# A fused Mamba and local-attention kernel: the time step by one Softplus activation

## The chip, the cores and the metric

The kernel runs on one core of one Trainium2 chip. The metric is the device time of one execution in microseconds, from launch to end; the profile's span is the stretch from the first to the last instruction inside it.

## The reference

Two branches read the same 4096 x 256 input and their results are added. The first is a Mamba block (inner width 512, 16 states, rank 16):

```
x_conv = silu(conv4(x @ in_proj_x) + conv_b);  z = x @ in_proj_z
dt_lr, B, C = split(x_conv @ x_proj.T)
dt  = softplus(dt_lr @ dt_proj_w.T + dt_proj_b)         # 4096 x 512
dA  = exp(dt * A);  dBx = (dt * x_conv) * B             # 4096 x 512 x 16
h_t = dA_t * h_(t-1) + dBx_t;  y_t = sum_n h_t * C_t
out = ((y + x_conv * D) * silu(z)) @ out_proj.T
```

The second is two layers of local attention (8 heads of 64, windows of 128 tokens, l2-normalised and rotated q and k, softmax) with a gated feed-forward of width 682 (gelu). Only the line that makes `dt` is computed in another way by the change.

## The kernel before

Everything is fp32. The 4096 tokens are worked in 8 chunks of 512. A chunk's Mamba state work is 64 units, one for each of 16 states and 4 tiles `j` of 128 channels (`NJ = 4`). A unit is a 128 x 512 tile: ScalarE makes `dA` = Exp(dt * A) (L963), VectorE makes dBx for two units at once (L749), runs the recurrence as one scan (L756) and multiplies two units by C (L763); GpSimd saves the last state (L1177) and issues a DMA that accumulates the product into `ysum` in HBM (L1193). `dA` is a ring of 8 tiles. Its tile is free for ScalarE's next Exp only when the accumulating DMA that reads it has landed (`act.wait_ge(*added[jb]...)`). `hb` is a ring of 4. The attention and feed-forward of the same chunk run between the units: 8 attention blocks `a` (2 layers x 4 windows) and 4 feed-forward halves `f`.

Each engine executes one fixed list in order. The lists are written out as strings: a FIRST list (chunk 0 and the start of chunk 1), an ORDER list that is run six times, and a LAST list; a word names a stage and its arguments, and each `+` says that it belongs to a later chunk. `heads(7)` is the transposition of q and k of attention block 7, `s` the scores (L1390 mask, L1396 product), `m` their row maximum on VectorE (L847), `e` the softmax exponentials on ScalarE (L1098), `turn` the rotation and norm (VectorE L824 to L842, ScalarE L1073), `h` the feed-forward's hidden tile (gelu L1130 on ScalarE, L899 on VectorE), `z` the Silu gate (L1144), `silu` the convolution's (L1019). TensorE writes into 7 PSUM banks taken in turn (`ring`); a bank is free when a named reader has read it.

The time step of a chunk passes through these stages:

- TensorE `xdbl` (L1351), ScalarE copy (L1033), TensorE `dt(j)` (L1358) into a PSUM bank.
- ScalarE `dt(j)` (L1038): dt_sb = Identity(PSUM + bias), which also frees the bank.
- VectorE `dt(half)` = `clip` (L805): u_sb = min(dt_sb, 40), for two tiles.
- ScalarE `softplus(half)`: an explicit load of a table that serves Exp and Ln (L1042), Exp in place on two tiles (L1045), Ln(x + 1) in place on two tiles (L1048).
- VectorE `u(half)`: dt_sb = max(dt_sb, u_sb) on two tiles (L811), then u_sb = dt_sb * x_conv (L816).
- The units of a half wait for `dt_ready` (ScalarE's Exp) and `u_ready` (VectorE's dBx).

Of the kernel before, what the change touches and what calls it, by code (L numbers as in the profile page):

```python
# [76 lines left out]
+k(3) +pT(2,0) +pT(2,1) +pT(2,2) +pT(2,3) +o(2,0) +o(2,1) +v(3) +hT(0) +o(2,2) +o(2,3) +h(0,0) +h(0,1)
+h(0,2) +h(0,3) +heads(3) +h(0,4) +h(0,5) +s(3,0) +s(3,1) +rb(2) ++xnT(0) +w2(0) ++xnT(1) +wo(2) +pT(3,0)
+pT(3,1) +pT(3,2) +x2T(0) +rb(3) +pT(3,3) +o(3,0) ++in(0) +o(3,1) ++in(1) ++in(2) +o(3,2) +o(3,3) ++in(3)
+q(4) +wo(3) +k(4) +sh(1) ++conv(0) ++conv(1) ++conv(2) ++conv(3) +heads(4) +hT(1) +q(5) +h(1,0) +h(1,1)  # L80
+h(1,2) +h(1,3) +h(1,4) +h(1,5) +s(4,0) +s(4,1) +k(5) +v(4) ++xdbl +w2(1) +pT(4,0) +rb(4) +pT(4,1) +pT(4,2)
# [9 lines left out]
+scan w2(3) ++norm(0) branch(1) +scan +scan +scan +scan +m(1,0) +m(1,1) +o(0) +m(1,2) +m(1,3) +scan +rinv(1)
+turn(q,2) +turn(k,2) +scan +scan +o(1) +wo(0) +u(1) +turn(q,3) +m(2,0) +wo(1) +m(2,1) +m(2,2) +m(2,3)
+stats(0) +scan ++norm(1) +turn(k,3) +scan +scan +scan +h(0,0) +h(0,1) +h(0,2) +h(0,3) +scan +scan +rinv(2)
+h(0,4) +h(0,5) +m(3,0) +m(3,1) +scan +o(2) +m(3,2) +m(3,3) +scan +scan +rinv(3) +w2(0) +scan +wo(2) +scan
+scan +scan +o(3) +scan +scan +wo(3) +turn(q,4) +turn(k,4) +stats(1) +scan +scan +scan +scan +scan +scan
+turn(q,5) +scan +scan +h(1,0) +h(1,1) +h(1,2) +h(1,3) +scan +h(1,4) +h(1,5) +m(4,0) +m(4,1) +scan +m(4,2)
+m(4,3) +turn(k,5) +rinv(4) +scan +scan +gate(0) +w2(1) +scan +scan +scan +scan ++dt(0) +m(5,0) +o(4)
+m(5,1) +m(5,2) +m(5,3) +scan +rinv(5) +turn(q,6) +turn(k,6) +scan +o(5) +scan +wo(4) +wo(5) +stats(2) +scan
+m(6,0) +m(6,1) +m(6,2) +m(6,3) +scan +scan +turn(q,7) +turn(k,7) +h(2,0) +h(2,1) +scan +rinv(6) +h(2,2)
+h(2,3) +scan +h(2,4) +scan +h(2,5) ++u(0) +scan  # L100
# [2 lines left out]
+dA heads(7) +dA v(7) e(7,0) e(7,1) e(7,2) e(7,3) +q(0) pT(7,0) pT(7,1) pT(7,2) pT(7,3) +k(0) +dA rb(7)
+turn(q,0) +turn(k,0) +v(0) +heads(0) +dA +dA +q(1) hn(3) +e(0,0) +e(0,1) +pT(0,0) +k(1) +e(0,2) +e(0,3)
last(3) hT(3) +dt(2) +dA +dA +dt(3) +dA +dA +dA h(3,0) h(3,1) h(3,2) +turn(q,1) h(3,3) h(3,4) h(3,5) +rb(0)
+start(0) +dA +dA +turn(k,1) +dA +dA +pT(0,1) +pT(0,2) +softplus(1) +dA +pT(0,3) +heads(1) +dA +dA +z(0)
# [1493 lines left out]
```

## Time and profile before

| | |
|---|---|
| median of 3 runs | 2244.7 us (2244.4 to 2245.45) |
| profiled execution, whole | 2240.71 us |
| its span | 2238.9 us |
| TensorE matmul busy | 2058.0 us (92%) |
| VectorE busy | 2016.8 us (90%) |
| ScalarE busy | 1680.9 us (75%) |
| GpSimd busy | 928.2 us (41%) |
| mean granted TensorE clock | 0.976 of full |

Busy time counts the union of an engine's instructions; waits are idle time. The matmul engine's ends are modelled, so its busy share is an upper view of its load. A row of a group of instructions gives the line, engine, operation, tiles and count, then busy us and mean ns of one, then the idle time just ahead of them and what ended it.

### The profile page before, as it was taken

How to read it: one execution, taken by the hardware profiler on the slowest of the kernel's cores; microseconds unless marked ns; L12 is line 12 of the kernel's file. 1: busy time of each engine (PE TensorE's matmuls, PEld its weight loads, DVE VectorE, ACT ScalarE, POOL GpSimd, SP SyncE). 2: the span in 40 equal slices, each digit the busy share in tenths (PEclk: the TensorE clock that was granted, in tenths of full speed). 3: DMA queues.
4: the chain of work that ended last, by engine and by line, in shares of the span. 5: the costliest groups of instructions: out<-in, count | busy, mean ns of one | idle time of the engine just before them, and what ended most of it. 6: DMA issues, size and time to landing. Idle time of an engine off the chain costs nothing. (4 is left out here: it accounts for less than half of the span.)

```text
span 2238.9 us, 37820 instructions
## 1 busy us (share of the span) xinstructions
PE 2058.0 (92%) x10944; PEld 1318.1 (59%) x10944; DVE 2016.8 (90%) x2804; ACT 1680.9 (75%) x4087; POOL 928.2 (41%) x1086
## 2 busy tenths in 40 slices
PE   6789989999899999999899998999989999898897
...
GB/s 142 145 152 194 188 155 183 180 205 175 161 196 178 188 161 157 220 187 169 193 136 189 208 187 165 157 179 200 181 166 196 173 197 167 163 162 217 115 200 54
DMA packets 113131, 388.52 MB, mean 174 GB/s; under 512 B 11408, under 2 KB 32272, under 8 KB 94368
## 3 DMA queue, kind: packets, MB, share of 16 engines
...
## 5 line engine op out<-in xcount | busy, mean ns | idle before, releaser
L756 DVE TENSOR_TENSOR_SCAN hb<-dA,state,hb 128x512 f32<-128x512 f32 x512 | 668.3, 1305 | 34.7 <-ACT dA L963 20.5
L1177 POOL COPY state<-hb 128x2 f32<-128x2 f32 x256 | 223.5, 873 | 638.5 <-DVE hb L756 638.2
L963 ACT ACTIVATE dA<-dt_sb,amat 128x512 f32<-128x512 f32 x512 | 344.3, 720 | 81.8 <-DMA ysum<-dA 80.8
L1193 POOL DMA_DIRECT2D ysum<-dA x256 | 220.2, 883 | 382.6 <-DVE dA L763 272.6
L1465 PE MATMUL ring<-hT,w 128*128 128x256 f32 (+1 forms) x1536 | 354.5, 388 | 17.4 <-ACT hT L1119 16.9
L1465 PEld LDWEIGHTS ring<-hT,w 128*128 128x128 f32 (+1 forms) x1536 | 272.6, 182 | 94.5 <-ACT hT L1119 26.0
L749 DVE TENSOR_TENSOR hb<-u_sb,bc 128x1024 f32<-128x1024 f32 x256 | 311.3, 1216 | 2.0 <-DMA bc<-bc_rows 1.9
L763 DVE TENSOR_TENSOR dA<-hb,bc 128x1024 f32<-128x1024 f32 x256 | 307.2, 1200 | 0.0
L1073 ACT ACTIVATE rot<-rot,rnorm 128x64 f32<-128x64 f32 x1024 | 257.2, 339 | 50.8 <-POOL rnorm L1262 50.7
L1098 ACT ACTIVATE probs<-ring,nmax 128x256 f32<-128x256 f32 x512 | 235.6, 483 | 55.5 <-DVE nmax L847 55.1
L1262 POOL TENSOR_TENSOR rnorm<-rnorm,powers 128x8 f32<-128x8 f32 x128 | 230.2, 1799 | 23.5 <-POOL rnorm L1259 23.5
L847 DVE TENSOR_REDUCE nmax<-ring 128x2 f32<-128x512 f32 x256 | 163.3, 681 | 41.9 <-PE ring L1396 41.6
L1477 PE MATMUL ring<-w,hid 128*128 128x256 f32 (+1 forms) x768 | 192.2, 395 | 0.3 <-issue 0.3
L1373 PE MATMUL ring<-wqkv,x2T 128*128 128x512 f32 x384 | 183.0, 606 | 9.6 <-ACT xconv L1019 9.0
L1106 ACT ACTIVATE pT<-ring 128x512 f32<-128x512 f32 x256 | 146.2, 598 | 53.6 <-PE heads_out L1417 28.1
L1373 PE MATMUL ring<-wqkv,xnT 128*128 128x512 f32 x384 | 181.6, 603 | 0.1
L1477 PEld LDWEIGHTS ring<-w,hid 128*128 128x128 f32 (+1 forms) x768 | 135.3, 189 | 55.4 <-issue 42.2
L1417 PE MATMUL heads_out<-pT,V 128*64 128x128 f32 x2048 | 152.7, 282 | 10.7 <-ACT pT L1106 5.6
L1316 PE MATMUL ring<-ident,probs 128*128 128x128 f32 x1024 | 142.1, 279 | 16.6 <-ACT probs L1098 6.9
L1396 PE MATMUL ring<-kT,qT 64*128 64x256 f32 x1024 | 156.0, 426 | 0.0
L1316 PEld LDWEIGHTS ring<-ident,probs 128*128 128x128 f32 x1024 | 115.2, 142 | 63.3 <-issue 41.5
L1417 PEld LDWEIGHTS heads_out<-pT,V 128*64 128x64 f32 x2048 | 110.9, 137 | 65.3 <-issue 64.6
...
## 6 DMA issues: line engine op xcount, KB each, us to landing
bc<-bc_rows SPq DMA_DIRECT2D x128, 1024.0 KB, 5.8
ysum<-dA POOLq DMA_DIRECT2D x256, 512.0 KB, 7.2
...
```

Of the source, the lines that this page charges most:

```text
L749: dve.tensor_tensor(hb[:, slot:slot + 2, :], u_pair, bc[:, g % 2, :, 0, :], ALU.mult)\
L756: dve.tensor_tensor_scan(hb[:, k % H_RING, :], dA[:, k % DA_RING, :], hb[:, k % H_RING, :], state[:, k:k + 1], ALU.mult, ALU.add).then_inc ...
L763: dve.tensor_tensor(dA[:, out:out + 2, :], hb[:, slot:slot + 2, :], bc[:, g % 2, :, 1, :], ALU.mult).then_inc(hC_ready.sem, 1)
L963: act.activation(dA[:, k % DA_RING, :], dt_sb[:, j, :], ACT.Exp, scale=amat[:, n:n + 1]).then_inc(dA_ready.sem, 1)
L1073: act.activation(rot[:, i, h * DH:(h + 1) * DH], rot[:, i, h * DH:(h + 1) * DH], ACT.Copy, scale=rnorm[:, i * HEADS + h:i * HEADS + h + 1] ...
L1098: act.activation(probs[:, g, odd, :], bank(it, ("s", a, p))[:, hh * 256:(hh + 1) * 256], ACT.Exp, bias=nmax[:, 2 * p + hh:2 * p + hh + 1], ...
L1262: pool.tensor_tensor(rnorm[:, part], rnorm[:, part], powers[:, part], ALU.pow).then_inc(rnorm_ready.sem, 1)
L1316: m = pe.transpose(bank(it, name)[:, b * P:(b + 1) * P], block_, ident[:, :])
L1373: m = pe.matmul(bank(it, name)[:, :], (x2T if l else xnT)[:, ft, off:off + WIN], wqkv[:, ft, i * 512:(i + 1) * 512], start=(ft == 0), stop ...
L1417: m = pe.matmul(obank[odd * DH:(odd + 1) * DH, g * WIN:(g + 1) * WIN], V[:, a // NW, s, h * DH:(h + 1) * DH], pT[:, g % 2, 2 * odd + s, :] ...
L1465: m = pe.matmul(bank(it, ("h", f, i))[0:rows, part * 256:(part + 1) * 256], w1[:, ft, col:col + rows], hT[:, ft, :], start=(ft == 0), stop ...
L1477: m = pe.matmul(bank(it, ("w2", f))[:, v * D:(v + 1) * D], hid[0:rows, i, v * WIN:(v + 1) * WIN], w2[0:rows, i, :], start=(i == 0), stop=( ...
```

## The change

`clip`, the Exp, the Ln, the maximum, the table load by hand and four of the five semaphores of the chain go. ScalarE's stage `dt(j)` now writes dt_sb = Softplus(PSUM + bias) and signals `dt_ready`; TensorE's bank is freed by that. VectorE's `u(half)` keeps only the product, and takes over the wait for the old chunk's last reader of `u_sb` that `clip` had. The function text no longer names a table; the build puts a table load in front of an activation whose function is not in the loaded table, as it does for the other activations before.

```diff
-            def clip(half):
-                for j in range(half * JH, half * JH + JH):
-                    dve.wait_ge(*dtv_ready.at(it, j + 1))
-                    dve.wait_ge(*dBx_ready.at(it - 1, (half + 1) * SUMS // HALVES))
-                    dve.tensor_scalar(u_sb[:, j, :], dt_sb[:, j, :], 40.0, None, ALU.min).then_inc(dtmin_ready.sem, 1)
-
             def u(half):
 
-                for j in range(half * JH, half * JH + JH):
-                    dve.wait_ge(*dtlog_ready.at(it, j + 1))
-                    dve.tensor_tensor(dt_sb[:, j, :], dt_sb[:, j, :], u_sb[:, j, :], ALU.max)\
-                       .then_inc(dt_ready.sem, 1)
                 for j in range(half * JH, half * JH + JH):
                     dve.wait_ge(*dt_ready.at(it, j + 1))
                     dve.wait_ge(*xconv_ready.at(it, j + 1))
+                    dve.wait_ge(*dBx_ready.at(it - 1, (half + 1) * SUMS // HALVES))
                     dve.tensor_tensor(u_sb[:, j, :], dt_sb[:, j, :], xconv[:, j, :], ALU.mult).then_inc(u_ready.sem, 1)
...
-            def dt_out(j):
+            def softplus(j):
                 act.wait_ge(*filled(it, ("dt", j)))
                 act.wait_ge(*dA_ready.at(it - 1, (j // JH + 1) * UNITS // HALVES))
-                act.activation(dt_sb[:, j, :], bank(it, ("dt", j))[:, :], ACT.Identity,
-                               bias=par[:, C_DTB + j:C_DTB + j + 1]).then_inc(dtv_ready.sem, 1)
-
-            def softplus(half):
-                act.preload_act_table_set("natural_log_exp_and_others")
-                for j in range(half * JH, half * JH + JH):
-                    act.wait_ge(*dtmin_ready.at(it, j + 1))
-                    act.activation(u_sb[:, j, :], u_sb[:, j, :], ACT.Exp).then_inc(dtexp_ready.sem, 1)
-                for j in range(half * JH, half * JH + JH):
-                    act.wait_ge(*dtexp_ready.at(it, j + 1))
-                    act.activation(u_sb[:, j, :], u_sb[:, j, :], ACT.Ln, bias=1.0).then_inc(dtlog_ready.sem, 1)
+                act.activation(dt_sb[:, j, :], bank(it, ("dt", j))[:, :], ACT.Softplus,
+                               bias=par[:, C_DTB + j:C_DTB + j + 1]).then_inc(dt_ready.sem, 1)
```

All fifteen order lists are written anew in the same diff: the same stages without the removed ones, in another order. The places that matter below, cut from them:

```diff
 ACT_ORDER (head)
-+dA heads(7) +dA v(7) e(7,0) e(7,1) e(7,2) e(7,3) +q(0) pT(7,0) pT(7,1) pT(7,2) pT(7,3) +k(0) +dA rb(7)
+heads(7) v(7) +dA +dA e(7,0) e(7,1) +q(0) e(7,2) e(7,3) +k(0) pT(7,0) pT(7,1) pT(7,2) pT(7,3) +dA rb(7)
...
 ACT_ORDER (the z gates)
-+start(0) +dA +dA +turn(k,1) +dA +dA +pT(0,1) +pT(0,2) +softplus(1) +dA +pT(0,3) +heads(1) +dA +dA +z(0)
-+z(1) +z(2) +z(3) +dA +dA +dA +e(1,0) +e(1,1) +e(1,2) +e(1,3) +q(2) +k(2) +v(1) +pT(1,0) +pT(1,1) +turn(q,2)
++pT(0,0) +dA +dA +dA +turn(q,1) +turn(k,1) +pT(0,1) +heads(1) +dA +dA +z(0) +pT(0,2) +dA +pT(0,3) +z(1)
++z(2) +z(3) +start(1) +dA +dA +dA +e(1,0) +e(1,1) +e(1,2) +e(1,3) +q(2) +pT(1,0) +k(2) +v(1) +pT(1,1)
...
 ACT_ORDER (tail)
-+h(2,0) +h(2,1) ++softplus(0) +h(2,2) +h(2,3) +h(2,4) +h(2,5) +pT(6,0) +pT(6,1) +dA +dA +pT(6,2) +turn(q,7)
-+rb(6) +turn(k,7) ++skip(0) +pT(6,3) ++dA ++dA
++e(6,3) +k(7) +pT(6,0) +turn(q,7) +turn(k,7) +h(2,0) +h(2,1) +h(2,2) +h(2,3) +rb(6) +h(2,4) +h(2,5) +dA +dA
+++dA ++skip(0) +pT(6,1) ++dA +pT(6,2) +last(2) +pT(6,3)
...
 PE_FIRST (head)
-xnT(0) xnT(1) in(0) in(1) in(2) in(3) conv(0) conv(1) conv(2) conv(3) q(0) xdbl dt(0) dt(1) k(0) heads(0)
+xnT(0) xnT(1) k(0) q(0) in(0) in(1) conv(0) conv(1) in(2) in(3) conv(2) conv(3) heads(0) xdbl q(1) dt(0)
...
 DVE_FIRST (head)
-norm(0) norm(1) +norm(0) turn(q,0) dt(0) +norm(1) turn(k,0) u(0) scan scan m(0,0) m(0,1) m(0,2) m(0,3) scan
+norm(0) norm(1) turn(q,0) turn(k,0) +norm(0) m(0,0) m(0,1) u(0) m(0,2) m(0,3) turn(q,1) scan scan rinv(0)
...
 ACT_FIRST (where dt is made)
-dt(0) dt(1) k(0) softplus(0) turn(k,0) dA heads(0) skip(0) dA dA +xn(0) dA dA e(0,0) e(0,1) e(0,2) pT(0,0)
+silu(1) xdbl q(1) heads(0) dt(0) dt(1) e(0,0) dA e(0,1) e(0,2) dA dA dA pT(0,0) dA dA dA e(0,3) v(0) z(0)
```

## Rows read from the trace of the kernel before

**Rows 1.** The page: the span, and busy us, share and count by engine.

```profile
span 2238.9 us, 37820 instructions
PE 2058.0 (92%) x10944; PEld 1318.1 (59%) x10944; DVE 2016.8 (90%) x2804; ACT 1680.9 (75%) x4087; POOL 928.2 (41%) x1086
```

**Rows 2.** Windows of five steady passes, cut at ScalarE's xdbl copies: total and mean busy.

```profile
sum 1341.50, PE 1270.85 PEld 814.51 DVE 1256.72 ACT 1044.35 POOL 575.51; mean PE 254.17 PEld 162.90 DVE 251.34 ACT 208.87 POOL 115.10
```

**Rows 3.** Groups by line in those five passes, matmul engine.

```profile
L1390 PE MATMUL ring<-mask,identb 128*128 128x512 bf16 x160 | 51.3, 404 | 25.1 <-ACT qT L1063 25.1
```

**Rows 4.** Groups by line in those five passes, VectorE.

```profile
L756 DVE TENSOR_TENSOR_SCAN hb<-dA,state,hb 128x512 f32<-128x512 f32 x320 | 417.3, 1304 | 21.3 <-ACT dA L963 12.4
L847 DVE TENSOR_REDUCE nmax<-ring 128x2 f32<-128x512 f32 x160 | 102.0, 681 | 26.1 <-PE ring L1396 25.8
```

**Rows 5.** Groups by line and form, VectorE, whole span.

```profile
L811 DVE TENSOR_TENSOR dt_sb<-dt_sb,u_sb 128x512 f32<-128x512 f32 x32 | 25.8, 846 | 0.2 <-ACT u_sb L1048 0.2
...
L805 DVE TENSOR_SCALAR u_sb<-dt_sb 128x512 f32<-128x512 f32 x32 | 11.8, 408 | 3.4 <-ACT dt_sb L1038 3.2
```

**Rows 6.** Groups by line and form, ScalarE, whole span.

```profile
L963 ACT ACT_TABLE_LOAD x55 | 70.6, 1283 | 1.0
L1130 ACT ACT_TABLE_LOAD x50 | 64.2, 1283 | 0.9
...
L1038 ACT ACTIVATE dt_sb<-ring,par 128x512 f32<-128x512 f32 x32 | 21.2, 692 | 1.0 <-PE ring L1358 0.8
L1042 ACT ACT_TABLE_LOAD x16 | 20.5, 1283 | 0.3
...
L1045 ACT ACTIVATE u_sb<-u_sb 128x512 f32<-128x512 f32 x32 | 18.4, 622 | 0.2
...
L1048 ACT ACTIVATE u_sb<-u_sb 128x512 f32<-128x512 f32 x32 | 18.1, 613 | 0.0
...
L1019 ACT ACT_TABLE_LOAD x8 | 10.3, 1283 | 0.1
L1144 ACT ACT_TABLE_LOAD x8 | 10.3, 1283 | 0.1
...
L1098 ACT ACT_TABLE_LOAD x3 | 3.8, 1283 | 0.1
L944 ACT ACT_TABLE_LOAD x1 | 1.3, 1283 | 8.3 <-POOL hid L1161 8.3
```

**Rows 7.** Timeline of the opening: start us, length us, instruction, idle ahead of it.

```profile
44.85 1.88 PE L1373 MATMUL ring<-wqkv,xnT 128*128 128x512 f32 x4
50.33 0.59 ACT L1033 ACTIVATE xdbl<-ring 48x512 f32<-48x512 f32 x1 [2.91 <-PE ring L1351]
55.58 1.28 ACT L1042 ACT_TABLE_LOAD   x1
56.87 1.15 ACT L1045 ACTIVATE u_sb<-u_sb 128x512 f32<-128x512 f32 x2
61.02 1.97 PE L1316 MATMUL ring<-ident,rot 128*128 128x128 f32 x8 [6.16 <-ACT rot L1073]
62.30 1.28 DVE L756 TENSOR_TENSOR_SCAN hb<-dA,state,hb 128x512 f32<-128x512 f32 x1
66.75 1.29 DVE L847 TENSOR_REDUCE nmax<-ring 128x2 f32<-128x512 f32 x2 [3.17 <-PE ring L1396]
```

**Rows 8.** Timeline at the head of a steady pass: ScalarE, matmul engine, VectorE.

```profile
1111.84 1.33 ACT L963 ACTIVATE dA<-dt_sb,amat 128x512 f32<-128x512 f32 x2 [3.27 <-DMA ysum<-dA]
1115.21 0.72 ACT L963 ACTIVATE dA<-dt_sb,amat 128x512 f32<-128x512 f32 x1 [2.04 <-DMA ysum<-dA]
1116.95 1.03 PE L1390 MATMUL ring<-mask,identb 128*128 128x512 bf16 x2 [5.71 <-ACT qT L1063]
1120.03 1.29 DVE L847 TENSOR_REDUCE nmax<-ring 128x2 f32<-128x512 f32 x2 [3.83 <-PE ring L1396]
```

**Rows 9.** Who waited for whom in those five passes: total us, times, longest.

```profile
ACT dA L963 <- DMA ysum<-dA: 61.7, 36, 4.1
```

More of the change, by code:

```diff
@@ L77 @@
[L77 to L81, printed above, removed]
@@ L91 @@
[L91 to L95, printed above, removed]
@@ L96 @@
[L96 to L100, printed above, removed]
++scan +scan w2(2) m(7,0) m(7,1) o(6) m(7,2) m(7,3) +scan +turn(q,0) rinv(7) +turn(k,0) wo(6) +scan o(7)
@@ L101 @@
++m(6,1) +m(6,2) +m(6,3) +scan +turn(q,7) +scan +turn(k,7) +scan +rinv(6) +scan +h(2,0) +h(2,1) +h(2,2)
++h(2,3) +scan +h(2,4) +h(2,5) +scan
 """
 ACT_ORDER = """
[L103 to L106 removed]
@@ new lines @@
++e(3,1) +e(3,2) +rb(2) +e(3,3) ++xnT(0) ++xn(1) ++xnT(1) +pT(3,0) +dA +pT(3,1) +pT(3,2) +pT(3,3) +rb(3) +dA
++dA ++in(0) ++in(1) +x2T(0) +dA +skip(1) +dA ++in(2) +dA +dA ++in(3) +q(4) +k(4) +dA +dA +turn(q,4)
++turn(k,4) +dA +dA +hn(1) ++silu(0) ++silu(1) +hT(1) +heads(4) +q(5) +dA +dA +dA +h(1,0) +h(1,1) +h(1,2)
++h(1,3) +h(1,4) +h(1,5) +dA +dA +dA +dA +e(4,0) +e(4,1) +e(4,2) +e(4,3) +k(5) +pT(4,0) +last(1) +dA +pT(4,1)
+++xdbl +dA +v(4) +turn(q,5) +turn(k,5) +dA ++dt(0) +heads(5) ++dt(1) +pT(4,2) +pT(4,3) +dA +dA +e(5,0)
@@ L162 @@
+h(1,0) scan scan h(1,1) h(1,2) h(1,3) h(1,4) h(1,5) scan scan m(4,0) m(4,1) m(4,2) m(4,3) scan scan w2(1)
+rinv(4) scan scan +u(0) m(5,0) m(5,1) m(5,2) m(5,3) scan turn(q,6) rinv(5) o(4) scan turn(k,6) scan scan
+wo(4) o(5) gate(0) scan wo(5) m(6,0) m(6,1) m(6,2) m(6,3) scan stats(2) rinv(6) turn(q,7) turn(k,7) scan
+scan scan scan h(2,0) h(2,1) h(2,2) h(2,3) scan h(2,4) h(2,5) scan
 """
 ACT_FIRST = """
-xn(0) xn(1) xnT(0) xnT(1) start(0) start(1) in(0) in(1) in(2) in(3) silu(0) silu(1) q(0) xdbl turn(q,0)
@@ L175 @@
-e(5,2) e(5,3) v(5) rb(4) dA q(6) dA k(6) pT(5,0) pT(5,1) pT(5,2) pT(5,3) +softplus(0) rb(5) turn(q,6)
-turn(k,6) last(2) heads(6) v(6) dA dA dA dA e(6,0) e(6,1) hn(2) e(6,2) pT(6,0) e(6,3) q(7) pT(6,1) hT(2)
-pT(6,2) k(7) turn(q,7) h(2,0) h(2,1) dA dA pT(6,3) h(2,2) h(2,3) h(2,4) h(2,5) dA dA +dA +dA turn(k,7)
-+skip(0) rb(6)
+xn(0) xn(1) xnT(0) xnT(1) in(0) q(0) k(0) start(0) in(1) start(1) turn(q,0) in(2) in(3) turn(k,0) silu(0)
+silu(1) xdbl q(1) heads(0) dt(0) dt(1) e(0,0) dA e(0,1) e(0,2) dA dA dA pT(0,0) dA dA dA e(0,3) v(0) z(0)
@@ new lines @@
+e(3,1) e(3,2) dA e(3,3) pT(3,0) pT(3,1) pT(3,2) pT(3,3) dA dA x2T(0) skip(1) rb(3) q(4) k(4) dA dA dA dA
+turn(q,4) dA dA dA turn(k,4) +silu(0) hn(1) +silu(1) hT(1) q(5) last(1) heads(4) k(5) h(1,0) dA dA dA dA dA
+v(4) h(1,1) h(1,2) h(1,3) h(1,4) h(1,5) turn(q,5) turn(k,5) dA dA dA +xdbl e(4,0) e(4,1) e(4,2) dA e(4,3)
+heads(5) +dt(0) +dt(1) x2T(1) rb(4) pT(4,0) dA pT(4,1) pT(4,2) dA e(5,0) e(5,1) q(6) pT(4,3) e(5,2) e(5,3)
+k(6) pT(5,0) v(5) dA dA rb(5) pT(5,1) pT(5,2) pT(5,3) turn(q,6) turn(k,6) v(6) heads(6) dA dA dA e(6,0)
@@ L179 @@
+e(6,1) e(6,2) e(6,3) dA q(7) k(7) pT(6,0) dA pT(6,1) pT(6,2) hn(2) pT(6,3) hT(2) dA rb(6) dA h(2,0)
+turn(q,7) turn(k,7) h(2,1) h(2,2) h(2,3) h(2,4) h(2,5) dA +dA +dA last(2) +skip(0)
 """
 POOL_FIRST = """
[L181 to L183 removed]
@@ new lines @@
++pT(0,1) +q(2) +k(2) +dA +dA +dA last(3) +dA +dA +heads(1) +dA +z(0) +turn(q,2) +turn(k,2) +z(1) +z(2) +z(3)
++pT(0,2) +dA +pT(0,3) +dA +dA +e(1,0) +e(1,1) +e(1,2) +e(1,3) +dA +heads(2) +start(0) +pT(1,0) +rb(0) +v(1)
++pT(1,1) +dA +dA +q(3) +k(3) +pT(1,2) +pT(1,3) +rb(1) +dA +dA +dA +dA +turn(q,3) +turn(k,3) +e(2,0) +e(2,1)
++last(0) +pT(2,0) +e(2,2) +e(2,3) +hn(0) +hT(0) +pT(2,1) +v(2) +dA +dA +dA +heads(3) +h(0,0) +h(0,1) +h(0,2)
++h(0,3) +h(0,4) +h(0,5) +dA +dA +dA +dA +pT(2,2) +pT(2,3) +e(3,0) +e(3,1) +e(3,2) +e(3,3) +skip(1) +dA
```

278 lines of the change are left out of this document (134 added, 144 removed).

## The prediction

> **What bounds the kernel now.** I read the page's busy line first [rows 1]: the matmul engine is busy 2058.0 us and VectorE 2016.8 us of 2238.9, so two engines carry the time almost equally, and ScalarE, which the change relieves too, has 25% idle. The chain that ended last is of little use here; it can be followed back only over the closing stretch, and no changed operation is on it. So I cut the steady part into windows at ScalarE's copy of xdbl, one for each pass of the ORDER list [rows 2]. Five passes take 1341.5 us, 268.3 each. In one the matmul engine works 254.2 (idle 14.1), VectorE 251.3 (idle 17.0), ScalarE 208.9 (idle 59.4). No engine is saturated. What the two near-full engines lack is lost in waits on one another through short chains in fixed lists.
>
> The largest of these waits has one place [rows 3, 4, 8]. Once in each pass the matmul engine waits for ScalarE's copy of qT, 25.1 us in five passes, or 5.0 each. The timeline shows why: ScalarE has `heads(7)` behind three `dA`, and these wait 3.27 and 2.04 us for the accumulating DMA that still reads their ring tile. The matmul engine stands 5.71 us, the scores come late, and VectorE stands 3.83 us for them. Over five passes ScalarE's waits on those DMAs are 61.7 us [rows 9]; elsewhere in the pass they fall into its idle time.
>
> **VectorE's part.** 32 clips of 408 ns and 32 maxima of 846 ns go: 11.8 + 25.8 = 37.6 us busy [rows 5], 4.7 us per chunk, 1.9% of VectorE's work. Their cost is plain in-order work: the idle time ahead of them is 3.6 us in the whole span. The product L816 stays. Its new wait for dBx of the old chunk is for VectorE's own earlier instructions in the same list, which clip had to wait for as well; I cost it at nothing. If it did bind, the unit loop behind it on VectorE would stand.
>
> What of the 4.7 us reaches the period? At most all: then VectorE works 246.6, and a period of 263.6 would hold the matmul engine at 96%, which its 14.1 us of idle time allows. At least nothing: where the matmul engine is the late one, VectorE's time only becomes waiting. The two have nearly equal load, so I take half, 2.35 us per pass.
>
> **ScalarE's part.** 32 Exp and 32 Ln go: 18.4 + 18.1 = 36.5 us. 32 Identity of 692 ns become 32 Softplus of an unknown price [rows 6]. The nearest bounds are the Ln, 613 ns, and the sum of the three that it replaces, 692 + 622 + 613 = 1927 ns. I take 692, the row with the same shapes, PSUM source and bias column. At 1927 ns ScalarE would win nothing in work, and VectorE's saving would stand.
>
> The Trainium skill (ScalarE: Activation LUTs, What ACT_TABLE_LOAD costs) states that an activation with a bias column costs about 280 ns plus 0.833 ns per element whatever the function; an estimate from that for 512 elements is 706 ns. The trace of before runs no Softplus and can't show it for this function.
>
> **Table loads.** I walked the lists (FIRST, six times ORDER, LAST) and put a load wherever the function's table was not the last one loaded, with Exp served by the table of L1042 as well. This gives 1 + 55 + 50 + 16 + 8 + 8 + 3 = 141, each the count in its row [rows 6], so the rule of placing is right for this kernel. For the new lists the same walk depends on where Softplus lives. With a table of its own it gives 146: 69 ahead of dA, 34 gelu, 17 Softplus, 15 ahead of `z` (the z gates are now split by a dA), 8 `silu`, 2 ahead of `e`, 1 first. That is 18 a pass instead of 17. If it shared Exp's table it would be 113. I take 146: 5 x 1.283 = 6.4 us more; the bounds are -28 x 1.283 = -35.9 and +6.4. Net, ScalarE loses 36.5 - 6.4 = 30.1 us of work, 3.8 per chunk. Since it is idle 59.4 us a pass, only what stands in front of a needed copy counts, and I book nothing for it except below.
>
> The row shows a load of 1283 ns after which the next activation starts 1.29 us behind the load's start [rows 7]. The Trainium skill (ScalarE: Activation LUTs, What ACT_TABLE_LOAD costs) adds a drain of some 1380 ns to each load, 2.66 us per switch. By the page the five further loads would cost 13.3 us of ScalarE instead of 6.4, still under its idle time; the trace shows no such drain.
>
> **The new lists.** All engines' lists are new, with no stage added. Most of that can't be costed from a trace; two places can.
>
> Head of a pass: `heads(7)` now stands ahead of the third dA, and the two others (`++dA`) have a skip, copies and `last(2)` between them. The third cost 2.04 + 0.72 = 2.76 us in front of the copy that both other engines stood for [rows 8]. Part of this comes back, since VectorE's scan needs that same dA soon. Between nothing and 2.76 I take 1.0 per pass.
>
> Opening: before, xdbl's copy starts at 50.33 and the first scan at 62.30, with the matmul engine standing 6.16 us for the rotation that ScalarE does behind its Exp, Ln and load, and VectorE 3.17 later for the scores [rows 7]. The new lists put k(0) (1.88 by the row of q) and heads(0) (1.97) ahead of xdbl, some 3.9 us later. From there, by the lengths that the same instructions have in that timeline: copy 0.6, q(1) in its shadow up to 1.9, dt 0.6, load 1.28, two Softplus 1.27, product 1.3, then two row maxima 1.3, turn(q,1) 2.9, dBx 1.2. The first scan would fall near 54.2 + 12.3 = 66.5, 4 us later, but VectorE has then done the four row maxima (2.6) and turn(q,1) (2.9), and doesn't stand 3.17 and more for the scores: 5.5 + 3.2 - 4.2 = 4.5, and the matmul engine is rid of up to 6.2. I take 5 us; the bounds are 0 and 9.
>
> **Sum.** Against the profiled execution: 2240.7 whole, 2238.9 span, 1.8 around it, and 4.0 below the median of the runs shown, so a difference is carried to the median as it stands. Seven passes x (2.35 + 1.0) = 23.5, with the opening 28.5: span 2210, execution 2212, median 2244.7 - 28.5 = 2216. The closing stretch is matmul work without dt and stays.
>
> **The rivals.**
>
> A. The forecast: about half of VectorE's saving reaches the period. 2204 to 2230, chance 0.50.
>
> B. The whole saving and the head of the pass arrive: 7 x (4.7 + 2.76) + 5 = 57 at most, and 7 x 4.7 + 5 = 38 with the first alone; 2188 to 2204. For it speaks that VectorE and the matmul engine stand together at the head of each pass; against it, that the matmul engine would then be at 97% or more. 0.15.
>
> C. The matmul engine is the bound and VectorE only waits longer: nothing from the passes, 0 to 9 from the opening, 2236 to 2245, middle 2240. For it speaks that it is the busier one, 254.2 against 251.3. Against it: it stands for VectorE's and ScalarE's results in every pass. 0.16.
>
> D. Slower: the accumulating DMA becomes the late one. A denser VectorE issues its sums in tighter groups, and each ScalarE dA waits for the landing of the sum eight units back; behind that dA stand the copies that the matmul engine needs. Before, this mechanism costs 5.0 us a pass at one place. A second such place in each pass adds 5.0 x 7 = 35 us and leaves, after the 28.5, 2251; two of them 2286. It decides from 28.5 / 7 = 4.1 us more per pass. 0.15.
>
> E. The change doesn't do what it says: Softplus costs 1927 ns, or takes a load for each tile. Then the dt chain is as long as before and dA of the half comes late, but VectorE's work is gone; a third of the forecast stays, 2235. 0.04.
>
> **How the numbers follow.** A measurement of this kernel can tell 0.2%, 4.5 us, from no change. Faster than 2240.2: A 0.50, B 0.15, half of C 0.08, E 0.04, together 0.77. Same: half of C, 0.08. Slower: D, 0.15. The range of 2196 to 2250 takes in A, C, E and half of B, and ends just below D. The likeliest case's own range is 2204 to 2230.
>
> **What the changed profile would show.** L805, L811, L1045, L1048 gone; VectorE busy near 2016.8 - 37.6 = 1979 us; a Softplus of 0.69 us; ScalarE near 1651, with 146 loads of 1283 ns (113 or another count tells the table); a period near 265; the matmul engine's busy time unchanged, its wait for qT at the head of the pass under 3 us. The prediction is wrong if the matmul engine's idle time in a pass doesn't fall: either VectorE's idle time grew by the 4.7 us (C), or ScalarE's waits for ysum did (D).

## The result, and the profile after

The changed kernel takes 2193.95 us (median of 4 runs, 2192.75 to 2198.5) against 2244.55 us of the kernel before measured beside it (4 runs, 2242.83 to 2245.45): a ratio of 0.9779 [0.9762, 0.9796], 50.6 us less. The forecast was 28.5 us less, 2216 us. The direction is right, the size is that of rival B, and the time lies 2 us under the range.

The page after, the span and the busy line, answers to [rows 1]:

```profile
span 2192.7 us, 37661 instructions
PE 2033.0 (93%) x10944; PEld 1318.7 (60%) x10944; DVE 1986.4 (91%) x2740; ACT 1651.2 (75%) x4028; POOL 946.4 (43%) x1086
```

VectorE has lost 30.4 us and ScalarE 29.7 us of work. The windows of the five steady passes, cut at the same copies as [rows 2]:

```profile
core 0: us, PE busy (x) PEld busy (x) DVE busy (x) ACT busy (x) POOL busy (x), PEclk, DMA share, GB/s
496.60:761.60 265.00, 252.40 (x1369) 163.12 (x1368) 247.71 (x341) 205.97 (x504) 118.61 (x134) 0.99 0.73 182
...
sum 1315.50, PE 1257.36 PEld 816.29 DVE 1239.40 ACT 1030.26 POOL 595.50; mean PE 251.47 PEld 163.26 DVE 247.88 ACT 206.05 POOL 119.10
```

A pass takes 263.1 us where it took 268.3. The five passes give 26.0 of the 46.2 us by which the span is shorter; what lies ahead of them (up to the third cut, 512.4 before and 496.6 after) gives 15.8, and the closing stretch 4.4 (385.0 against 380.6). In a pass the matmul engine now stands 11.6 us (14.1 before) and VectorE 15.2 (17.0 before).

The granted clock has a part in the difference. Its mean is 0.976 over the span before and 0.984 after, and the loss lies in short stretches in which it is 0.50, the 1.2 GHz level, and not 1.00, the 2.4 GHz level. One of them stood at the head of each of the five steady passes of the kernel before, right behind the matmul engine's wait for `qT` (3.5 to 6.4 us long). In the changed kernel that wait is 0.15 us in each pass and the clock stays at 1.00 there. First before, behind the 5.71 us of [rows 8]: the window, and the scores product in it; then the same place after:

```profile
1116.00:1122.00 6.00, 5.05 (x18) 2.39 (x20) 1.48 (x3) 2.65 (x7) 0.75 (x2) 0.50 1.03 268
1117.92 2.08 PE L1396 MATMUL ring<-kT,qT 64*128 64x256 f32 x8
```

```profile
1094.00:1100.00 6.00, 5.85 (x37) 3.12 (x36) 3.50 (x7) 4.79 (x13) 1.05 (x2) 1.00 0.85 226
1095.20 0.61 PE L1365 MATMUL ring<-mask,identb 128*128 128x512 bf16 x2 [0.15 <-ACT qT L1038]
1095.74 1.14 PE L1371 MATMUL ring<-kT,qT 64*128 64x256 f32 x8
```

The eight scores products take 2.08 us at the lower level and 1.14 at the upper. Read in windows of 1 us, the five passes before hold some 31 us at 0.50 (27 of them at the heads) and after some 10 us. Half of that is lost against the upper level: 15.3 and 5.1 us, so at most 10.2 of the 26.0 us. How much of it reached the time, no run isolates.

ScalarE by line and form, whole span, the rows that answer to [rows 6]:

```profile
L947 ACT ACT_TABLE_LOAD x69 | 88.5, 1283 | 1.2
L1105 ACT ACT_TABLE_LOAD x34 | 43.6, 1283 | 0.6
L1022 ACT ACT_TABLE_LOAD x17 | 21.8, 1283 | 0.3
L1022 ACT ACTIVATE dt_sb<-ring,par 128x512 f32<-128x512 f32 x32 | 21.2, 687 | 0.5 <-PE ring L1333 0.2
L1119 ACT ACT_TABLE_LOAD x15 | 19.2, 1283 | 3.9 <-PE ring L1309 3.7
L1003 ACT ACT_TABLE_LOAD x8 | 10.3, 1283 | 0.1
L1073 ACT ACT_TABLE_LOAD x2 | 2.6, 1283 | 0.0
L928 ACT ACT_TABLE_LOAD x1 | 1.3, 1283 | 8.3 <-POOL hid L1136 8.3
```

Softplus costs 687 ns. The seven groups of loads are 146, and each count is the one that the walk through the lists gave for a Softplus with a table of its own.

VectorE by line in the five passes, which answers to [rows 4]:

```profile
L750 DVE TENSOR_TENSOR_SCAN hb<-dA,state,hb 128x512 f32<-128x512 f32 x321 | 418.2, 1303 | 8.2 <-ACT dA L947 0.9
...
L832 DVE TENSOR_REDUCE nmax<-ring 128x2 f32<-128x512 f32 x160 | 101.9, 683 | 20.1 <-PE ring L1371 20.1
```

The scan's wait for `dA` has gone from 12.4 to 0.9 us in five passes. The waits of the whole span, after and then before (total us, times, longest):

```profile
ACT dA L947 <- DMA ysum<-dA: 82.8, 44, 5.9
```

```profile
ACT dA L963 <- DMA ysum<-dA: 80.8, 48, 4.1
PE ring L1390 <- ACT qT L1063: 30.4, 8, 6.4
DVE hb L756 <- ACT dA L963: 20.5, 17, 3.7
```

After, the wait for `qT` is 2.4 us in all and the scan's for `dA` 2.6, although ScalarE waits as long as before for accumulating DMAs. These waits no longer stand in front of something that is needed at once. The rest of the text asks what brought that about.

### The profile page after: what moved, and what is told of

Read it like the earlier page. It is cut to its first block and busy times, and to the rows that moved or that the text cites. A ratio compares the mean times of both kernels' runs of the same rounds, so it can differ in the third digit from the quotient of the medians.

```text
span 2192.7 us, 37661 instructions
## 1 busy us (share of the span) xinstructions
PE 2033.0 (93%) x10944; PEld 1318.7 (60%) x10944; DVE 1986.4 (91%) x2740; ACT 1651.2 (75%) x4028; POOL 946.4 (43%) x1086
## 5 line engine op out<-in xcount | busy, mean ns | idle before, releaser
L1152 POOL COPY state<-hb 128x2 f32<-128x2 f32 x256 | 242.7, 948 | 391.2 <-DVE hb L750 390.2
L947 ACT ACTIVATE dA<-dt_sb,amat 128x512 f32<-128x512 f32 x512 | 344.8, 718 | 84.0 <-DMA ysum<-dA 82.8
L1440 PE MATMUL ring<-hT,w 128*128 128x256 f32 (+1 forms) x1536 | 354.7, 388 | 11.6 <-ACT hT L1094 11.0
L1440 PEld LDWEIGHTS ring<-hT,w 128*128 128x128 f32 (+1 forms) x1536 | 272.7, 182 | 84.8 <-ACT hT L1094 20.5
L743 DVE TENSOR_TENSOR hb<-u_sb,bc 128x1024 f32<-128x1024 f32 x256 | 308.4, 1205 | 10.2 <-DMA bc<-bc_rows 7.9
L757 DVE TENSOR_TENSOR dA<-hb,bc 128x1024 f32<-128x1024 f32 x256 | 314.2, 1227 | 0.0
L1237 POOL TENSOR_TENSOR rnorm<-rnorm,powers 128x8 f32<-128x8 f32 x128 | 234.6, 1833 | 24.4 <-POOL rnorm L1234 24.0
L1348 PE MATMUL ring<-wqkv,xnT 128*128 128x512 f32 x384 | 189.4, 625 | 0.0
L1392 PE MATMUL heads_out<-pT,V 128*64 128x128 f32 x2048 | 148.0, 281 | 7.5 <-ACT pT L1081 2.8
L1371 PE MATMUL ring<-kT,qT 64*128 64x256 f32 x1024 | 146.2, 405 | 0.0
## 6 DMA issues: line engine op xcount, KB each, us to landing
w<-in_w SPq DMA_DIRECT2D x16, 1364.0 KB, 11.8
```

The lines of the kernel that those rows point to most:

```text
L743: dve.tensor_tensor(hb[:, slot:slot + 2, :], u_pair, bc[:, g % 2, :, 0, :], ALU.mult)\
L757: dve.tensor_tensor(dA[:, out:out + 2, :], hb[:, slot:slot + 2, :], bc[:, g % 2, :, 1, :], ALU.mult).then_inc(hC_ready.sem, 1)
L947: act.activation(dA[:, k % DA_RING, :], dt_sb[:, j, :], ACT.Exp, scale=amat[:, n:n + 1]).then_inc(dA_ready.sem, 1)
L1152: pool.tensor_copy(state[:, 2 * m:2 * m + 2], hb[:, slot:slot + 2, T - 1]).then_inc(state_saved.sem, 1)
L1348: m = pe.matmul(bank(it, name)[:, :], (x2T if l else xnT)[:, ft, off:off + WIN], wqkv[:, ft, i * 512:(i + 1) * 512], start=(ft == 0), stop ...
L1392: m = pe.matmul(obank[odd * DH:(odd + 1) * DH, g * WIN:(g + 1) * WIN], V[:, a // NW, s, h * DH:(h + 1) * DH], pT[:, g % 2, 2 * odd + s, :] ...
```

## The experiments

Ratios are to the kernel before on the same chip, with 95% intervals; "pass" is the mean length of the five steady passes, 268.3 us before and 263.1 after. The edits are shown cut to the lines that matter, most without their semaphores.

### Functions alone, lists alone

**Functions alone**: the new functions; the lists of before with the removed stages struck out and nothing else moved.

```diff
 DVE_ORDER (one of the places)
-branch(0) h(3,0) +scan +scan h(3,1) +rinv(0) +dt(1) h(3,2) h(3,3) h(3,4) h(3,5) +scan +scan +scan +scan
+branch(0) h(3,0) +scan +scan h(3,1) +rinv(0) h(3,2) h(3,3) h(3,4) h(3,5) +scan +scan +scan +scan
 ACT_ORDER (one of the places)
-+pT(0,2) +softplus(1) +dA
++pT(0,2) +dA
```

> The new functions (one Softplus per tile, no clip, Exp, Ln, maximum) under the order lists of before, from which only the removed stages are struck. Whole VectorE saving arrives (37.6 us) and the lists matter little: 2205 to 2210. The forecast's terms (half of VectorE's saving, nothing from ScalarE): 2226 to 2230. New lists do most of it: 2236 to 2243, since these are the old ones.

2273.15 us, 1.013 [1.0108, 1.0153]; pass 272.7. **Slower** than before, with VectorE at 1989.3 us busy. The table loads are 167 instead of 141.

**Lists alone**: the old functions under the new lists, with the removed stages put back by hand (128 loads).

```diff
 DVE_ORDER
-+scan h(3,0) h(3,1) h(3,2) h(3,3) +scan
++scan h(3,0) h(3,1) h(3,2) h(3,3) +dt(1) +scan
...
 ACT_ORDER
-+dA +turn(q,1) +turn(k,1) +pT(0,1)
++dA +turn(q,1) +turn(k,1) +softplus(1) +pT(0,1)
```

> The functions of before (clip, Exp, Ln, maximum, table load by hand) under the new order lists, with the removed stages put back between the Softplus place and the product. Whole VectorE saving is the cause: 2235 to 2246, no gain from lists. The forecast's terms (opening 5, head of pass 1.0 a pass): 2232. New lists do most of it: 2205 to 2215.

2253.07 us, 1.0043 [1.0024, 1.0063]; pass 270.8. The wait for `qT` is down to 7.2 us in the whole span and the scan's for `dA` to 13.7, and still nothing is won. So neither half of the change makes the kernel faster alone; together they give 50.6 us. My hand placement may be a part of this result.

### Putting the work back, under the new lists

**VectorE's work back**: the changed kernel with a minimum and a maximum per tile ahead of the product, written to `u_sb`, which the product overwrites.

```diff
+                    dve.tensor_scalar(u_sb[:, j, :], dt_sb[:, j, :], 40.0, None, ALU.min)
...
+                    dve.tensor_tensor(u_sb[:, j, :], dt_sb[:, j, :], u_sb[:, j, :], ALU.max)
```

> The changed kernel, with VectorE's 32 minima and 32 maxima back in front of the products, reading dt_sb and writing only u_sb, so that ScalarE's path stays short: pure VectorE work, and the output is the same. VectorE's work reaches the span whole: 2194 + 37 = 2231. Half of it: 2213. Matmul engine is the bound: 2194 to 2198.

2217.48 us, 0.9888 [0.9863, 0.9914]; pass 267.0; VectorE busy 2016.5. 30.1 us of work cost 23.5 us of time.

**ScalarE's work back**: four Exp of the PSUM bank into `dt_sb` ahead of each half's first Softplus, which overwrites them. Each waits for the one before it. The Exp and Ln of the kernel before stood in a place of their own, so this is work of the same amount, not quite in the same place.

```diff
+                if j % JH == 0:
+                    for i in range(2 * JH):
+                        act.activation(dt_sb[:, j + i % JH, :], bank(it, ("dt", j))[:, :], ACT.Exp)
```

> The changed kernel, with four extra Exp from PSUM in front of the first Softplus of each half (their results are overwritten), in all 64 of about 0.6 us, the ScalarE work that the change removed. ScalarE's 59 us of idle time a pass hides them: 2194 to 2199. ScalarE's relief or the shorter chain to dt is the cause of what the forecast lacked: 2210 or more.

2213.54 us, 0.9868 [0.9845, 0.9891]; pass 266.2; ScalarE busy 1681.2, with one table load more (147). 30.0 us of work cost 19.6 us on an engine that has 57 us idle in each pass. It did not cost it at the scan, whose wait for `dA` is 3.2 us in the whole span (2.6 in the changed kernel). What came late are the copies that stand behind this stage in ScalarE's list: the matmul engine's waits for `qT` grew from 2.4 to 9.5 us, for the z gates from 2.8 to 9.9, for V from 1.4 to 4.5. One place, ScalarE and then the matmul engine:

```profile
1042.44 2.01 ACT L1026 ACTIVATE dt_sb<-ring 128x512 f32<-128x512 f32 x4
1044.47 1.28 ACT L1029 ACT_TABLE_LOAD   x1
```

```profile
1047.48 0.60 PE L1372 MATMUL ring<-mask,identb 128*128 128x512 bf16 x2 [1.92 <-ACT qT L1045]
1048.02 1.93 PE L1378 MATMUL ring<-kT,qT 64*128 64x256 f32 x8
```

Here too the granted clock falls to 0.50 behind the wait (1.93 us for the eight products), and its mean in this profile is 0.975 against 0.984. That the Exp hold the PSUM bank longer is not the cost: the matmul engine waits 0.5 us for it in the whole span.

**ScalarE's work back, away from the dt stage**: xin's copies and z's gates are made twice. The second of each pair waits for the first. The xin copies are not wholly off the way to dt: they feed the convolution from which `xdbl` and then dt are made, some stages earlier.

```diff
+                act.activation(xin[:, j, TAPS - 1:], bank(it, ("xin", j))[:, :], ACT.Copy)
...
+                act.activation(sz[:, j, :], bank(it, ("z", j))[:, :], ACT.Silu)
```

> The changed kernel with ScalarE's copies of xin and its z gates each made twice, 64 activations of about 0.6 us that are not on the way to dt; the output is the same. If the fourth run's 20 us were the price of ScalarE work wherever it stands: 2210 to 2215. If they were the longer way to dt: 2194 to 2199.

2205.34 us, 0.9829 [0.9813, 0.9845]; pass 263.8. 36.0 us of work cost 11.4 us, and 8.7 of them are lost before the third cut (505.3 against 496.6). The result lies between the two expectations, with most of the loss ahead of the steady passes. In a steady pass 4.5 us of such work cost 0.7, where in front of the Softplus 3.8 us cost 3.1. So in a steady pass idle time does cover this work of ScalarE's, but not work in front of the Softplus and the copies behind it; the wait for `qT` is 2.8 us here.

### The table loads

**Shared table**: Exp in the place of Softplus, so dt is an exponential; the loads fall from 146 to 113.

```diff
-                act.activation(dt_sb[:, j, :], bank(it, ("dt", j))[:, :], ACT.Softplus,
+                act.activation(dt_sb[:, j, :], bank(it, ("dt", j))[:, :], ACT.Exp,
```

> The changed kernel with Exp in the place of Softplus (dt is exp instead of softplus): 113 loads instead of 146, lists the same. Loads hidden under ScalarE's idle time: 2190 to 2196. Loads on the path at their length or a good part of it (33 x 1.28 = 42 us): 2160 to 2180.

2191.63 us, 0.9763 [0.9731, 0.9795]; pass 263.3. 33 loads fewer (42 us of ScalarE) bring 2 us, inside the intervals.

**The same under the old lists**: functions alone, with this edit (dt again an exponential); 122 loads instead of 167.

> The first experiment's kernel (new functions, old lists) with Exp in the place of Softplus, so that dt shares dA's table: 122 loads instead of 167, and dt is exp instead of softplus. If the 26 loads more than before (141) are what made that kernel slower than before, this one falls below before, to 2215 to 2230, as the forecast had it for the removed work. If the old lists are unfit for another reason (copies and dA that now come at the wrong time), it stays at 2255 or more.

2243.7 us, 0.9991 [0.9969, 1.0013]; pass 269.2. Here the 45 loads are worth 29.5 us. Functions alone was slow by its loads; and even without them it only ties with the kernel before, though VectorE is rid of 26 us. Where that went, the waits show:

```profile
ACT dA L948 <- DMA ysum<-dA: 106.3, 47, 5.5
DVE hb L751 <- ACT dA L948: 40.7, 19, 5.5
```

The scan's wait for `dA` has doubled (20.5 before), and ScalarE's for the accumulating DMA grew by 25.5.

### The head of the pass

**Before, heads first**: one place in the ORDER list of ScalarE.

```diff
-+dA heads(7) +dA v(7) e(7,0) e(7,1)
+heads(7) v(7) +dA +dA e(7,0) e(7,1)
```

> The kernel before with one edit in the repeated ScalarE list: heads(7) and v(7) ahead of the two dA at the head of the pass. The forecast's term: 1.0 us in each of six passes, 2238; its upper bound 2.76 a pass, 2228. If a list can't be edited at one place without the others: within 0.3% of before or slower.

2224.19 us, 0.9902 [0.9873, 0.993]; pass 264.8. The head is worth 3.5 us a pass. The waits after the edit:

```profile
ACT dA L963 <- DMA ysum<-dA: 74.7, 49, 4.2
PE ring L1390 <- ACT qT L1063: 16.7, 7, 4.4
```

**After, with that undone**:

```diff
-heads(7) v(7) +dA +dA e(7,0) e(7,1) +q(0)
++dA heads(7) +dA v(7) e(7,0) e(7,1) +q(0)
```

> The changed kernel with that edit undone (a dA ahead of heads(7), one between it and v(7)). The forecast's term: 1.0 us a pass back, 2200; upper bound 2211. If the head of the pass has no such wait any more: 2194 to 2196.

2195.86 us, 0.9778 [0.9749, 0.9807]; pass 263.5. Nothing is lost. What is worth 3.5 us a pass in one kernel is worth nothing in the other. The `dA` again stands in front of what both engines need, but in this run's timeline (1092.83 us) it has no wait for a DMA, and the matmul engine waits 0.44 us for `qT`. In the changed lists GpSimd issues that sum (`add(28)`) ahead of a turn and a save; what that is worth, the part on the late sum shows.

**Heads first, VectorE's work gone**: clip and maximum struck out of that kernel, Exp and Ln kept; Ln writes `dt_sb`.

```diff
-                    act.wait_ge(*dtmin_ready.at(it, j + 1))
-                    act.activation(u_sb[:, j, :], u_sb[:, j, :], ACT.Exp)
+                    act.wait_ge(*dtv_ready.at(it, j + 1))
+                    act.activation(u_sb[:, j, :], dt_sb[:, j, :], ACT.Exp)
...
-                    act.activation(u_sb[:, j, :], u_sb[:, j, :], ACT.Ln, bias=1.0)
+                    act.activation(dt_sb[:, j, :], u_sb[:, j, :], ACT.Ln, bias=1.0)
```

> The kernel before with heads(7) first (2224 as measured, 0.990 of before) and VectorE's clip and maximum struck: ScalarE's Exp reads dt_sb and writes u_sb, its Ln writes dt_sb. ScalarE's work and its 141 loads stay. If the wait at the head of the pass had swallowed VectorE's saving in the old lists, it now arrives: 2224 less 20 to 33, so 2191 to 2204. If the old lists are bound by something else: 2220 to 2226.

2224.66 us, 0.9912 [0.9886, 0.9939]; pass 264.8, as without it. VectorE's busy time falls from 2017.8 to 1990.7 and not one microsecond arrives:

```profile
DVE hb L756 <- ACT dA L959: 32.6, 22, 5.4
ACT dA L959 <- DMA ysum<-dA: 78.2, 46, 4.6
```

The scan's wait for `dA` was 16.2 us in the kernel with the work. VectorE arrives earlier and finds `dA` not there.

**Heads first, functions new, Exp for Softplus** (dt is again an exponential): the kernel of "functions alone", with these two edits.

```diff
-+dA heads(7) +dA v(7) e(7,0) e(7,1)
+heads(7) v(7) +dA +dA e(7,0) e(7,1)
...
-                act.activation(dt_sb[:, j, :], bank(it, ("dt", j))[:, :], ACT.Softplus,
+                act.activation(dt_sb[:, j, :], bank(it, ("dt", j))[:, :], ACT.Exp,
```

> New functions, old lists with heads(7) first, Exp in the place of Softplus (dt is exp instead of softplus; 122 loads). VectorE's and ScalarE's work both gone, no loads added. Against the fifth run (2244, without heads first) this gives the head of the pass for the new functions: 22 less as in the kernel before gives 2222; if the head hid the savings, 2190 or less. Against the ninth it gives ScalarE's part.

2225.09 us, 0.9912 [0.9883, 0.9941]; pass 264.1. Both engines are relieved, ScalarE to 1624.1 us, and again nothing arrives.

**Functions alone, mended**: the new functions with Softplus, heads first, and `dt(3)` moved next to `dt(2)` on ScalarE and the matmul engine, to save 12 loads.

```diff
 ACT_ORDER
-last(3) hT(3) +dt(2) +dA +dA +dt(3) +dA +dA +dA h(3,0)
+last(3) hT(3) +dt(2) +dt(3) +dA +dA +dA +dA +dA h(3,0)
```

> New functions with Softplus under the old lists, heads(7) first and dt(3) moved next to dt(2) in the repeated lists of ScalarE and of the matmul engine: 155 loads. If loads between dt and dA and the head of the pass are all that was wrong with the old lists, this reaches 2195 to 2210, near the changed kernel; if the new lists are needed as a whole, 2230 or more.

2275.93 us, 1.0145 [1.0128, 1.0162]; pass 272.1. A miss, and slower than functions alone (2273.15). The scan's wait for `dA` doubled (32.9 us in functions alone), and ScalarE now stands for the store of the output, and behind it the `dA`:

```profile
DVE hb L751 <- ACT dA L948: 66.7, 28, 5.5
ACT X L953 <- DMA out_y<-X: 33.8, 6, 6.4
```

### The late sum

Something else held `dA` under the old lists. The head's `dA` waits until 1111.84 for an accumulating DMA [rows 8]. Its product, and GpSimd's issue of that DMA, in the timeline of the kernel before:

```profile
1086.43 1.20 DVE L763 TENSOR_TENSOR dA<-hb,bc 128x1024 f32<-128x1024 f32 x1
```

```profile
1084.19 0.99 POOL L1177 COPY state<-hb 128x2 f32<-128x2 f32 x1 [1.26 <-DVE hb L756]
1095.07 0.99 POOL L1177 COPY state<-hb 128x2 f32<-128x2 f32 x1 [9.89 <-DVE hb L756]
...
1096.59 1.68 POOL L1262 TENSOR_TENSOR rnorm<-rnorm,powers 128x8 f32<-128x8 f32 x1 [0.18 <-POOL rnorm L1259]
...
1099.32 2.42 POOL L1262 TENSOR_TENSOR rnorm<-rnorm,powers 128x8 f32<-128x8 f32 x1 [0.18 <-POOL rnorm L1259]
1101.69 1.87 POOL L1193 DMA_DIRECT2D ysum<-dA  x2
```

The product is ready at 1087.63. GpSimd, 41% busy, issues its sum at 1101.69: in its list `add(28)` stands behind a save of the state, which waits 9.89 us for a scan that has not run yet, and behind two turns. That is 14.1 us in which the ring tile of the next chunk's first `dA` is held for nothing. I tried it by one word:

```diff
 POOL_ORDER (before)
-+add(27) +q(7) +scan +scan +turn(q,7) +turn(k,7) +add(28) +add(29)
++add(27) +q(7) +scan +add(28) +scan +turn(q,7) +turn(k,7) +add(29)
```

> The kernel before with one edit in GpSimd's repeated list: add(28) ahead of the state save and the two turns it stood behind. If the late sum is what holds the head of the pass: the first dA no longer wait, heads(7) comes early without being moved, 2218 to 2228, as much as the seventh run gained. If ScalarE's order was the cause and the sum is innocent: 2240 to 2246.

2213.31 us, 0.9864 [0.985, 0.9879]; pass 263.4. **One word in the kernel before gives 31 us**, and a pass as short as that of the changed kernel. The matmul engine now waits 1.5 to 2.7 us at the heads of the five passes, and the clock stays at its upper level there but for a part of one. The issue now follows its product, and `dA` at the head has no wait for the first two, 1.43 us for the third:

```profile
1079.84 0.99 POOL L1177 COPY state<-hb 128x2 f32<-128x2 f32 x1 [1.26 <-DVE hb L756]
1083.94 0.90 POOL L1193 DMA_DIRECT2D ysum<-dA  x1 [3.11 <-DVE dA L763]
```

```profile
1104.10 1.34 ACT L963 ACTIVATE dA<-dt_sb,amat 128x512 f32<-128x512 f32 x2
1106.86 0.72 ACT L963 ACTIVATE dA<-dt_sb,amat 128x512 f32<-128x512 f32 x1 [1.43 <-DMA ysum<-dA]
```

**Before, both words**: heads first and the sum early.

```diff
 ACT_ORDER
-+dA heads(7) +dA v(7)
+heads(7) v(7) +dA +dA
 POOL_ORDER
-+scan +scan +turn(q,7) +turn(k,7) +add(28) +add(29)
++scan +add(28) +scan +turn(q,7) +turn(k,7) +add(29)
```

> The kernel before with heads(7) first and add(28) early. One cause behind both edits: 2218 to 2226, no more than either alone. Two separate waits: 2200 to 2210.

2205.12 us, 0.9821 [0.9805, 0.9838]; pass 262.9. By the ratios 40 us, where the two edits alone sum to 53 (22 + 31): in part they remove the same stall.

**Both words, VectorE's work gone**: as above, with clip and maximum struck by the same diff as in "heads first, VectorE's work gone".

> The fourteenth run's kernel with VectorE's clip and maximum struck as in the ninth (ScalarE's work stays). If the late sum swallowed VectorE's saving, it now arrives: 12 to 30 us under the fourteenth run. If the old lists are bound elsewhere (matmul engine): within 5 us of it.

2201.21 us, 0.9808 [0.9793, 0.9823]; pass 261.5. 29 us less of VectorE's work (2013.5 to 1984.5) bring 3.9 us, and the intervals overlap, so it may be nothing. The scan's wait for `dA` takes a part again, 11.8 to 17.5.

**Both words, functions new, Softplus**: "functions alone" with both words moved (167 loads).

> The new functions with Softplus under the old lists (167 loads) with heads(7) first and add(28) early. If the loads between dt and dA under the old lists cost the 29 us that the first and fifth run showed, wherever the head of the pass is: 2201 + 29 = 2230, so the new lists are needed to place Softplus. If the loads cost only because the head was late: 2195 to 2205.

2239.78 us, 0.9981 [0.9963, 0.9999]; pass 266.0. Under the old lists Softplus gives back what the two words had won: it costs 38.6 us against the run above, at the same busy time of VectorE (1984.4) and nearly the same of ScalarE (1683.1 against 1680.3). So it is not how much ScalarE has to do. What differs is the number and the place of the loads (167 against 141), whose price under these lists the pair above showed (45 loads, 29.5 us). That this is the whole of the 38.6 us is not shown: the same kernel with Exp for Softplus was not run, and the mean granted clock differs as well, 0.972 against 0.979.

**The changed kernel with its sum late**: the word moved the other way.

```diff
 POOL_ORDER (after)
-+turn(q,7) +add(27) +add(28) +turn(k,7) +add(29) +scan
++turn(q,7) +add(27) +turn(k,7) +scan +add(28) +add(29)
```

> The changed kernel with add(28) and add(29) put behind turn(k,7) and a state save in GpSimd's repeated list. If the early sum is what lets the saving arrive: 2205 or more. If the new lists don't depend on it (heads(7) stands ahead of the dA there): 2193 to 2198.

2193.34 us, 0.9779 [0.9761, 0.9797]; pass 263.0. No loss. Behind one save and one turn, with `heads(7)` in front on ScalarE, the sum is not on the path. Each of the two words was moved back alone; a changed kernel with both moved back, which would show whether either one suffices, was not run.

**The changed kernel with its sums still earlier**: `merge(0)` behind two sums and two turns, `add(24)` and `add(27)` each ahead of a save.

```diff
-+q(4) +merge(0) +add(16) +add(17) +turn(q,4) +turn(k,4) +scan
++q(4) +add(16) +add(17) +turn(q,4) +turn(k,4) +merge(0) +scan
...
-+scan +scan +scan +add(24) +add(25)
++scan +scan +add(24) +scan +add(25)
...
-+stats(2) +scan +q(7) +turn(q,7) +add(27) +add(28)
++stats(2) +add(27) +scan +q(7) +turn(q,7) +add(28)
```

> The changed kernel with three edits in GpSimd's repeated list: merge(0) behind the sums 16 and 17 and two turns, add(24) ahead of a state save, add(27) ahead of a save, q(7) and turn(q,7). ScalarE's dA of unit 40 waits 5.3 us a pass for the landing of sum 16. If late sums still hold the pass: 2170 to 2188. If they only fill ScalarE's idle time now, since VectorE waits for dA 2.6 us in the whole span: 2190 to 2197.

2195.59 us, 0.9785 [0.9755, 0.9815]; pass 262.6. ScalarE's waits for the DMAs fall from 82.8 to 55.4 us and the time stays. What is left of them is not on the path.

## Why the prediction was off, step by step

- **The sum.** 28.5 us forecast, 50.6 measured. The counts and prices of the parts were right but for 7 us of VectorE's; what they are worth in the period was not.
- **Prices.** Right: Softplus 687 ns (692 taken), 146 loads, ScalarE 1651.2 us busy (1651). VectorE came to 1986.4, not 1979: its 256 products with C take 1227 ns where they took 1200, 7 us in all; why, I did not test.

- **"ScalarE's part: I book nothing."** This step failed. ScalarE has 59 us idle in a pass, and I took idle time for cover. Putting back 30.0 us in front of the Softplus costs 19.6, 3.1 of 3.8 us in a pass; elsewhere 0.7 of 4.5. The cover is real for the work put elsewhere, and absent in front of the Softplus: the copies of q, k and V and the z gates stand behind it in the list, and the matmul engine waits for them (for `qT` 9.5 us against 2.4). The forecast had said that only what stands in front of a needed copy counts, and then looked for it at the head of the pass alone. The Exp were put back in one place; what those of the kernel before cost in theirs is known only by this stand-in.
- **"I take half, 2.35 us per pass" for VectorE.** This term was mis-sized: its work put back costs 23.5 us, 3.4 for each of seven passes, where the forecast had 2.35 and 16.5 in all. A share is the wrong form too. The same saving is worth nothing with heads first, 0 to 4 us with both words, and 23.5 under the new lists. In the runs in which it doesn't arrive, the scan waits longer for `dA` (16.2 to 32.6 us, 11.8 to 17.5).
- **The head of the pass, 1.0 us (bounds 0 to 2.76).** The place was right, the cause one step short, the bound too low. I stopped at the accumulating DMA and asked what ScalarE's list had behind it. I did not ask why the DMA landed so late. It was issued 14.1 us after its data, by an engine that is 41% busy. Moving heads alone gives 3.5 us a pass, moving the sum 4.9. The bound of 2.76 took in only the third `dA`. The matmul engine's wait there was 5.0 us a pass, and I had left the clock out: behind that wait the masks and scores ran at 1.2 GHz, 6.0 us for what takes 3.3 in the changed kernel. Over the five heads it lost 13.6 us so, 2.7 a pass. This is what the kernel before lost; under the new lists either word undone alone costs nothing.
- **The opening, 5 us.** Low. Up to the third cut 15.8 us are won; one pass of 5.2 is in it, so about 10.6 belong to the opening and the first chunk. The parts in the timeline after:

```profile
50.32 0.59 ACT L1017 ACTIVATE xdbl<-ring 48x512 f32<-48x512 f32 x1 [3.75 <-PE ring L1326]
53.88 1.28 ACT L1022 ACT_TABLE_LOAD   x1
55.18 1.26 ACT L1022 ACTIVATE dt_sb<-ring,par 128x512 f32<-128x512 f32 x2
```

```profile
55.74 1.29 DVE L832 TENSOR_REDUCE nmax<-ring 128x2 f32<-128x512 f32 x2 [21.20 <-PE ring L1371]
...
63.37 1.28 DVE L750 TENSOR_TENSOR_SCAN hb<-dA,state,hb 128x512 f32<-128x512 f32 x1
```

  xdbl's copy is at 50.32, where it was at 50.33 [rows 7], and not 3.9 later: `k(0)` and `heads(0)` fit into time in which the matmul engine had stood. The first scan is at 63.37, 3.1 ahead of my 66.5.
- **Loads.** "5 x 1.283 us more, hidden" holds under the new lists (33 loads fewer: 2 us, inside the intervals). Under the old ones 45 loads are worth 29.5 us. The Trainium skill (ScalarE: Activation LUTs, What ACT_TABLE_LOAD costs) adds a drain of some 1380 ns to each load. The trace shows none: the Softplus starts 1.30 us behind the load's start, which is the load itself.
- **Rival D.** Its mechanism is real and swallowed VectorE's saving under the old lists, but as a wait in the saving's place, not as a loss beyond it. Under the new lists ScalarE's waits for the DMAs are as long as before (82.8 against 80.8) and do not decide. **Rival C** falls: with the matmul engine as the bound, putting VectorE's work back would have cost nothing. The sign named for C and D did not show either: the matmul engine's idle time in a pass fell, 14.1 to 11.6 us. **Rival E** falls by the 687 ns.
- **Rival B** has the number: its range of 2188 to 2204 holds the measured time. Its account is another: the whole of VectorE's saving, the head of the pass, and nothing for ScalarE. That the number fits is in part luck. Its smaller sum, 38 us, gives 2207 and lies outside its own range.
- **The matmul engine's busy time**, expected unchanged, is 25 us less with the same 10944 instructions. The clock, which the forecast did not look at, is a part of it and may be most: a mean of 0.976 over 2238.9 us is 54 us short of the upper level, 0.984 over 2192.7 is 35, so up to 19 of the 25 us (an estimate, since the engine stood idle in a part of the slow stretches). The scores product shows it in the rows of the two pages, a mean of 405 ns after and 426 before, at the same least time of 375 and 376 ns:

```profile
L1371 PE MATMUL ring<-kT,qT 64*128 64x256 f32 x1024 | 146.2, 405 | 0.0
```

```profile
L1396 PE MATMUL ring<-kT,qT 64*128 64x256 f32 x1024 | 156.0, 426 | 0.0
```

  So the 254.2 us in a pass of 268.3 were not all work at full speed, and the argument against rival B from that load was weaker than I took it.

**What is shown**: the new functions under the old lists are slower than the kernel before (1.013), the old functions under the new lists too (1.0043, with my placement), and together they give 0.9779. Work of ScalarE's in front of the Softplus and of VectorE's in front of the product costs time under the new lists (19.6 and 23.5 us when put back, each alone), and the old lists lost 31 us by one late sum. **What stays open**: how the last 7 to 11 us between the kernels with both words (2205 and 2201) and the changed kernel divide; how much of the lists-alone result is my placement, since the two works put back sum to 43 us (both at once was not run) and lists alone lies 59 above the changed kernel; how much of each difference is the lower clock behind a wait and how much the wait; and what a `dA` ring of more than 8 tiles would give, which was not tried.

None of these versions beats the changed kernel by more than the measurement tells. The nearest that computes the same is the one with the late sum, 2193.34 against 2193.95.
